# Expert batches of 6, 5, 3 and 2 groups in units of 128 rows, with the first layer's weights of a unit copied by ScalarE

## What is computed

```python
def _L0_gnn_ref(z, dist_matrix, W, B):
    msg = z @ W + B
    sens = exp(-(1.0 / r - 1.0 / MU) ** 2 / (2.0 * SIGMA ** 2))       # r = dist_matrix
    return where(dist_matrix < CUTOFF, sens, 0.0) @ msg

def _L0_ffn_ref(x, gate_w, gate_b, w1, b1, w2, b2, gamma, beta):      # H, F, E, K = 128, 256, 16, 2
    topk_vals, topk_idx = top_k(x @ gate_w + gate_b, K)
    topk_w = softmax(topk_vals, axis=-1)
    h = relu(einsum('bsh,ehf->bsef', x, w1) + b1)
    expert_out = einsum('bsef,efh->bseh', h, w2) + b2
    y = x + sum(topk_w * expert_out[topk_idx])
    return layernorm(y) * gamma + beta

x = x + _L0_gnn_ref(layernorm(x), adj, W, B)
x = x + _L0_ffn_ref(layernorm(x), ...)
```

## Time and profile before

| what | value |
|---|---|
| median of 3 runs | 1759.18 us (1758.34 to 1759.6) |
| the profiled execution | 1758.88 us, span 1757.1 us |
| PE busy | 1624.8 us, 92% |
| DVE busy | 1525.8 us, 87% |
| ACT busy | 1581.2 us, 90% |
| POOL busy | 430.1 us, 24% |
| HBM traffic | 194 GB/s over the span |

### The profile page before, as it was taken

The page is one execution under the profiler, slowest core; times in us unless marked ns, Lnnn a source line. Parts: engine busy times, 40 slices in busy tenths (PEclk is TensorE's granted clock), DMA queues, the critical chain, the costliest instruction groups (busy, mean ns, idle before and its releaser), DMA issues.

```text
span 1757.1 us, 23405 instructions
## 1 busy us (share of the span) xinstructions
PE 1624.8 (92%) x8178; PEld 1080.6 (61%) x8178; DVE 1525.8 (87%) x2278; ACT 1581.2 (90%) x1577; POOL 430.1 (24%) x309
## 2 busy tenths in 40 slices
PE   4889999999999999999999999999999999999840
PEld 3556666566656566656556656566656557999840
DVE  7999999999999999999999999999999994557876
ACT  5889999999999999999989999999999995666752
POOL 0000030303131313131304030303031301117775
PEclk9999999999999999999999999999999999999985
DMA  9447876667666666666867666667666842457653
GB/s 319 146 136 252 251 213 205 187 203 217 200 203 199 195 204 204 202 200 201 230 192 207 203 207 204 189 202 216 203 188 203 230 123 77 149 156 227 193 152 97
DMA packets 208500, 341.91 MB, mean 195 GB/s; under 512 B 18224, under 2 KB 65840, under 8 KB 208256
## 3 DMA queue, kind: packets, MB, share of 16 engines
q1 hardware_dynamic: 200064, 323.30, 61.9%
q0 software_dynamic: 8320, 17.12, 3.2%
HBM read 304.38 MB, written 35.98 MB: 194 GB/s over the span
## 4 chain that ended last, share of the span: by engine, by line
PE 44%; ACT 28%; DVE 12%; issue 11%; POOL 4%; DMA 1%; POOLq 0%; SPq 0%; DVEq 0%; ACTq 0%
PE acc L1033 22%; PE tp L1052 11%; ACT chunk L467 10%; ACT chunk L462 9%; ACT wT L473 8%; PE tp L1082 4%; PE tp L1095 4%; POOL chunk L446 4%; DVE chunk L595 4%; DVE chunk L589 4%; PE tp L1071 1%; PE misc L985 1%; DVE stats L601 1%; DVE msg L650 1%; DMA xs<-in_x_dram 1%
## 5 line engine op out<-in xcount | busy, mean ns | idle before, releaser
L1033 PE MATMUL acc<-wT,msg 128*128 128x512 f32 x2048 | 973.0, 598 | 16.2 <-DVE yT L681 16.2
L595 DVE SCALAR_TENSOR_TENSOR chunk<-chunk 128x2048 f32<-128x2048 f32 x256 | 585.6, 2287 | 98.2 <-ACT chunk L467 98.0
L1052 PEld LDWEIGHTS tp<-ident,chunk 128*128 128x128 f32 x4096 | 484.1, 142 | 226.2 <-issue 214.7
L473 ACT ACTIVATE wT<-tp 128x1024 f32<-128x1024 f32 x512 | 570.4, 1114 | 22.4 <-PE tp L1052 22.4
L589 DVE SCALAR_TENSOR_TENSOR chunk<-chunk 128x2048 f32<-128x2048 f32 x256 | 584.0, 2282 | 1.9 <-DMA chunk<-in_adj_dram 1.9
L1052 PE MATMUL tp<-ident,chunk 128*128 128x128 f32 x4096 | 538.5, 275 | 0.0
L462 ACT ACTIVATE chunk<-chunk 128x2048 f32<-128x2048 f32 x256 | 514.9, 2011 | 11.9 <-DVE chunk L589 11.9
L1033 PEld LDWEIGHTS acc<-wT,msg 128*128 128x128 f32 x2048 | 351.6, 192 | 267.7 <-issue 267.0
L467 ACT ACTIVATE chunk<-chunk 128x2048 f32<-128x2048 f32 x256 | 513.7, 2007 | 0.0
L418 POOL TENSOR_TENSOR pool_carrier<-pool_carrier 1x1 f32<-1x1 f32 x32 | 8.6, 270 | 1232.0 <-DVE row_now L766 1189.5
L428 POOL DMA_INDIRECT rows_in<-y,row_now x128 | 286.6, 2239 | 44.7 <-issue 44.7
(11 more groups left out here) (106 smaller groups left out, 574.8 us busy)
## 6 DMA issues: line engine op xcount, KB each, us to landing
chunk<-in_adj_dram SPq DMA_DIRECT2D x256, 1024.0 KB, 5.3
chunk<-rows_in SPq DMA_DIRECT2D x88, 128.0 KB, 2.1
rows_out<-chunk SPq DMA_DIRECT2D x88, 128.0 KB
y_kept<-y SPq DMA_DIRECT2D x16, 256.0 KB, 6.1
rows_in<-zeros SPq DMA_DIRECT2D x32, 128.0 KB
chunk<-y_kept SPq DMA_DIRECT2D x16, 256.0 KB, 3.4
out_dram<-chunk SPq DMA_DIRECT2D x16, 256.0 KB, 2.6
blobs<-in_L_ffn_w_dram SPq DMA_DIRECT2D x1, 2048.0 KB, 12.0
```

The source lines that it names most:

```text
L473: act.activation(wT[:, (g * PPG + m) % WSLOTS, :], tp[(g * PPG + m) % TSLOTS][:, :], ACT.Exp, scale=-2.0).then_inc(weighted, 1)
L595: dve.scalar_tensor_tensor(out=slot(c), in0=slot(c), scalar=2.0, in1=slot(c), op0=ALU.subtract, op1=ALU.mult).then_inc(squared, 1)
L1033: ins = pe.matmul(acc[:, :], msg[:, n, :], wT[:, (g * PPG + m) % WSLOTS, k * ROWS:(k + 1) * ROWS], start=(n == 0), stop=(n == 2 * PPG - 1))
L1052: ins = pe.transpose(tp[s % TSLOTS][:, t * ROWS + b * P:t * ROWS + (b + 1) * P], chunk[:, c % RING, b, j:j + P], ident[:, :])
```

## The change

There are four batches, of 6, 5, 3 and 2 groups, all in units of 128 rows, and a batch has 15 more units than its rows fill: 63, 55, 39 and 31, in all 188. There are three tables in the main phase, beside groups 7, 12 and 15. A unit's weights come to its slot by two engines: ACT copies the 256 columns of the first layer (`fetch_first`), DVE the other 386. Both run five units ahead, in 7 slots. PE's `hidden` waits for ACT's copy (`first_full`), `output` and ACT's `relu_hidden` for DVE's. There are 12 buffers for rows and 6 for results where there were 8 and 4. The gate's steps lie two units apart, and a combine begins every 11 iterations: 77, 88, 99, 110, 121, 132, 143, 154, 165, 176, 187, then 198, 209, 220, 231 and 242 with no units beside them.

```diff
-    BATCHES = (8, 6, 2)
-    TILES = (2, 2, 1)
+    BATCHES = (6, 5, 3, 2)
+    TILES = (1, 1, 1, 1)
...
-    UNITS = [K * n * ROWS // u + E for n, u in zip(BATCHES, UR)]
+    UNITS = [K * n * ROWS // u + E - 1 for n, u in zip(BATCHES, UR)]
...
-        SLOTS, RIN, RT, HT, RO, BACK, ZS, FIN = 4, 8, 3, 3, 4, 4, 3, 2
+        SLOTS, RIN, RT, HT, RO, BACK, ZS, FIN = 7, 12, 3, 3, 6, 4, 3, 2
...
-        GATE_PACE = 1
-        TABLE_AT, PADS_AT = 28, 47
+        GATE_PACE = 2
+        TABLE_AT, PADS_AT = 55, 74
         TAIL_TABLES = len(BATCHES) - 1
-        COMBINE_WAIT, COMBINE_PACE, COMBINE_LONG = 8, 6, 10
+        COMBINE_WAIT, COMBINE_PACE, COMBINE_LONG = 14, 11, 10
...
-                starts.append(max(at, starts[-1] + pace) if starts else at)
+                starts.append(max(at, starts[-1] + COMBINE_PACE) if starts else at)
...
+            def fetch_first(u):
+                b = batch_of(u)
+                if u == 0:
+                    act.wait_ge(weights_in, EXPERT_DMAS * 16)
+                if u == UNIT0[b]:
+                    act.wait_ge(table_ready, 2 * b + 2)
+                if u == UNIT0[b] or u % AT_ONCE == 0:
+                    upper = min(u // AT_ONCE * AT_ONCE + AT_ONCE, UNIT0[b + 1])
+                    _, values = nc.values_load_multi_w_load_instructions(
+                        e_tab[0:1, u:upper], engines=[mybir.EngineType.Activation], min_val=0, max_val=E - 1,
...
+                if u >= SLOTS:
+                    act.wait_ge(hid_full, u - SLOTS + 1)
+                act.activation(slots[u % SLOTS][:, W1:W1 + F], blobs[:, bass.ds(first_layers[u], 1), W1:W1 + F].rearrange("p a f -> p (a f)"),
+                               ACT.Copy).then_inc(first_full, 1)
...
                 act.wait_ge(hid_full, u + 1)
+                act.wait_ge(slot_full, u + 1)
...
+            for u in range(SLOTS - 2):
+                fetch_first(u)
             copy_rows(0)
...
                     relu_hidden(i + 1)
+                if i + SLOTS - 2 < NU:
+                    fetch_first(i + SLOTS - 2)
...
-                dve.tensor_copy(slots[u % SLOTS], blobs[:, bass.ds(experts[u], 1), :].rearrange("p a f -> p (a f)")).then_inc(slot_full, 1)
+                dve.tensor_copy(slots[u % SLOTS][:, W2:BLOB], blobs[:, bass.ds(experts[u], 1), W2:BLOB].rearrange("p a f -> p (a f)")).then_inc(slot_full, 1)
...
-                if i + 2 < NU:
-                    fetch(i + 2)
+                if i + SLOTS - 2 < NU:
+                    fetch(i + SLOTS - 2)
...
-                pe.wait_ge(slot_full, u + 1)
+                pe.wait_ge(first_full, u + 1)
...
                 pe.wait_ge(hT_ready, u + 1)
+                pe.wait_ge(slot_full, u + 1)
```

More of the change, by code:

```diff
@@ L211, in gnn_moe_kernel @@
         slot_full = sem("slot_full")
+        first_full = sem("first_full")
         hid_full = sem("hid_full")
@@ L230, in gnn_moe_kernel @@
         SETUP_MISC = 2
-        def batch_at(i):
-            return max(b for b in range(len(BATCHES)) if UNIT0[b] <= i)
-        GATE_PACE = 1
-        TABLE_AT, PADS_AT = 28, 47
+        GATE_PACE = 2
+        TABLE_AT, PADS_AT = 55, 74
         TAIL_TABLES = len(BATCHES) - 1
-        COMBINE_WAIT, COMBINE_PACE, COMBINE_LONG = 8, 6, 10
+        COMBINE_WAIT, COMBINE_PACE, COMBINE_LONG = 14, 11, 10
         starts = []
@@ L243, in gnn_moe_kernel @@
                 at = UNIT0[b + 1] + COMBINE_WAIT
-                pace = COMBINE_PACE if starts and UR[batch_at(starts[-1])] > P else COMBINE_LONG
-                starts.append(max(at, starts[-1] + pace) if starts else at)
+                starts.append(max(at, starts[-1] + COMBINE_PACE) if starts else at)
         LAST = starts[-1] + COMBINE_LONG + 2
@@ L433, in results_there @@
                 for i in range(RO):
-                    pool.wait_ge(ro_out[i], UNIT0[b + 1] // RO * 16)
+                    pool.wait_ge(ro_out[i], (UNIT0[b + 1] - i + RO - 1) // RO * 16)
             for b, n in enumerate(BATCHES):
@@ L520, in _ @@
                         guess(c + 3, (c + 3) % 2)
+            first_layers = {}
+            def fetch_first(u):
[8 more added lines that the diff above has]
+                        e_tab[0:1, u:upper], engines=[mybir.EngineType.Activation], min_val=0, max_val=E - 1,
+                        skip_runtime_bounds_check_because="a count of experts, clamped to the last one")
+                    first_layers.update(zip(range(u, upper), values))
+                if u >= SLOTS:
+                    act.wait_ge(hid_full, u - SLOTS + 1)
+                act.activation(slots[u % SLOTS][:, W1:W1 + F], blobs[:, bass.ds(first_layers[u], 1), W1:W1 + F].rearrange("p a f -> p (a f)"),
+                               ACT.Copy).then_inc(first_full, 1)
             def copy_rows(u):
@@ L551, in combine_slot @@
                     ins.then_inc(zn_ready, 1)
+            act.wait_ge(turned, (GROUPS - 1) * PPG + PPG - RING // 2 * PAIRS)
+            for u in range(SLOTS - 2):
+                fetch_first(u)
             copy_rows(0)
@@ L947, in _ @@
             dve.wait_ge(turned, (GROUPS - 1) * PPG + PPG - RING // 2 * PAIRS)
-            for u in range(2):
+            for u in range(SLOTS - 2):
                 fetch(u)
```

## The result

The changed kernel took 1770.37 us in the median of five runs (1766.69 to 1771.55) against 1759.18 (five runs too, 1757.78 to 1759.76): ratio 1.0059, 95% interval 1.0045 to 1.0074. It is **slower**, by 11.2 us between the medians and by 10.4 us by the ratio. The forecast was 1755.3, a little faster; 1770.37 lies within its range, which went up to 1772, but the change of direction was not forecast. The profiled execution spans 1768.4 us, 11.3 more than before.

What follows compares the result with a forecast made beforehand. ACT was taken to bound the main phase, the units' pace the two chains after it. Main phase +4.5, units 0.0, combines -8.4 sum to -3.9 us: 1755.3 us against 1759.18, range 1743 to 1772.

Steps and rivals of the forecast that it cites:

- SP's pace in the unit stage: Unit stage, SP's loads and stores: 1.07 us a unit up to iteration 77, then 1.25 beside combines.
- SP's queue is the bound: Rival, unit stage: SP's slack is used up early, 1.12 then 1.32 us a unit, 1767 us, slower; chance 0.20.
- 224.3 us: Unit stage: 188 units take what 120 took before, no gain and no loss.
- Main phase: Before the unit stage: one more table in a full group costs 4.5 us, bounds 3 and 6.
- Combines: Behind the last unit: six groups instead of seven, 53.5 us instead of 61.9, 8.4 us less.
- The new copy: Unit stage, ACT's copy of 256 first-layer columns: 0.31 us, making 0.97 us of ACT a unit.
- The dear copy: Rival, unit stage: ACT's copy of 256 columns costs 0.385 us or more, 1767 us, slower; chance 0.10.
- ACT alone paces: Rival, unit stage: SP's loads run ahead, ACT sets 1.03 then 1.20 us a unit, 1747 us; chance 0.25.
- The change does not do what it says: Rival, unit stage: ACT's copies precede its relus, PE's clock falls to 1.2 GHz, 40 us or more; chance 0.03.
- POOL: Gathers beside the combines: POOL alone would end at 1734 us, so it has come off the path.
- Table loads: Unit stage: 0.7 us for each of ACT's fifteen; loads last 1.1 us in the median on DVE and SP.

Runs made afterwards that it cites:

- everything that won: Changed kernel with paired stores, last batch's pads on POOL, all 642 columns fetched by DVE, a combine every 9 iterations: 1881.11, 1879.96 and 1880.9 us on slower chips.

## Why the prediction was wrong, point by point

- **The step that failed: SP's pace in the unit stage.** 1.00 us for store and load was right, and so was the order of the extras. But I took 1.07 us a unit for the first 77, on the ground that about 4 us of slack would carry half of the loss (SP's own sum was 1.12), and 1.25 beside combines, by spreading 16 pads, table loads and combine DMAs evenly over 110 units. Measured by DVE's adds, with the fill, the stage's first 77 iterations took 91.7 us where the forecast had 86.8 (+4.9), the other 110 took 151.7 for 137.5 (+14.2); together the 19.0. SP's slack did carry the first units: from the first add to the 41st it is 44.4 us, and 44.6 with SP relieved. DVE first waits for a store at 1522.90 us, for unit 42, and by the 77th add the changed kernel is 5.9 us behind the relieved one (89.1 for 83.2). Pads come one to a unit in a row: units 80 to 100 took 33.8 us, of which 20 x 1.25 = 25 were forecast, so 8.8 of the 14.2 lie in that fifth. Without the pads the same 20 units took 25.2. Six result buffers do not even that out: DVE waits as soon as six stores are behind. More of them were not tried.
- **The rival that came true** is the one that named this place: "SP's queue is the bound", 1767 us, 0.20. It had 1.12 and 1.32; measured, from the first add to the 77th, 1.17 (89.1 / 76, in which 2.5 us for the gate's products and the first gather lie too) and then 1.38 (151.7 / 110). Its condition was wrong: it was to decide only from 1.04 us for store and load on, and it decided at 1.00, by the extras. Its mechanism (pads, table loads and long issues together, DVE waiting for a result buffer) is what the waits show; for the stage it was 7.5 us short.
- **That 224.3 us came after all is luck.** With SP relieved the stage took 224.6 us, with 1.09 us a unit before combines (83.2 / 76, again with the gate's products) and 1.26 beside them (138.8 / 110). But the forecast's 1.07 and 1.25 were made from SP's cost, which is cut by 0.3 us a unit there. With SP out of the way the prediction's own sum for ACT alone is 210.3 + 5.5 = 215.8 us, 8.8 less than measured, and without ACT's copy the stage still took 221.9. So the terms behind SP were too low as well. ACT was busy for over 19 us in five of the eleven windows of 20 us from 1480 to 1700; how the 8.8 us divide among ACT, DVE, the rings and the table loads is open.
- **Main phase**: +4.5 forecast, +1.1 measured. With the change, the windows of the two groups with tables and of the last one, from one group's L703 copy to the next:

```profile
676.39:769.50 93.11, 88.36 (x398) 53.55 (x399) 88.53 (x103) 88.08 (x68) 19.08 (x9) 0.96 0.67 194
...
1118.74:1210.81 92.07, 86.66 (x399) 53.65 (x399) 87.52 (x103) 87.90 (x68) 19.07 (x9) 0.98 0.70 202
...
1385.24:1471.86 86.62, 84.67 (x382) 51.65 (x382) 69.66 (x99) 76.34 (x65) 11.24 (x9) 0.98 0.42 120
```

and of the last group before:

```profile
1381.11:1470.65 89.54, 85.05 (x384) 51.27 (x383) 70.13 (x97) 74.74 (x60) 9.91 (x9) 0.98 0.48 136
```

The two groups near 92 us came as said. The last is 2.9 us shorter. It is so in all versions with these batches (86.62, 86.63, and 85.71 with units of 256 rows), but with the old batches and ACT's copy (the run at 1806 us) it was 87.84, so up to 1.7 of the 2.9 us do not go with the batches. And 1.2 us are there at the first group (its L703 at 153.22 us, L681 at 154.44 before), ahead of anything that was changed. The +1.1 is not firm: in three profiles of one kernel, that with everything that won, the unit stage starts at 1468.99, 1473.74 and 1474.20 us. All profiles with units of 128 rows throughout have it below the 1475.4 of the forecast, so the term was too high, by how much is not known.
- **Combines**: -8.4 forecast, -8.8 measured, 8.4 us each, and the last waits for no gather. Right.
- **The new copy**: 0.31 us forecast. ACT's timeline (L535 is the copy, L544 the next row copy): 1499.85 to 1500.16 is 0.31. A whole unit, 1499.16 to 1500.16, is 1.00 without a wait that the profile shows, where the sum had 0.97; so ACT has no room there either. The dear copy falls. The Trainium skill's formula (ScalarE: Activation LUTs, section What ACT_TABLE_LOAD costs) gives an estimated 0.31 for it too: by that formula, the trace agrees.

```profile
1499.16 0.28 ACT L544 ACTIVATE chunk<-tp 128x128 f32<-128x128 f32 x1
1499.34 0.63 ACT L554 ACTIVATE chunk<-tp,chunk 128x128 f32<-128x128 f32 x2
1499.85 0.42 ACT L535 ACTIVATE chunk<-blobs 128x256 f32 x1
1500.16 0.28 ACT L544 ACTIVATE chunk<-tp 128x128 f32<-128x128 f32 x1
```

- **ACT alone paces** (0.25): it would have needed SP to run ahead, and SP did not. With SP relieved it was still too low, as said.
- **The change does not do what it says** (0.03): the granted clock was 1.00 in most windows of 20 us and 0.91 in two. Each of those two holds one short stretch at half speed, the 1.2 GHz level, from about 1592 and from about 1622 us on. Ahead of the first PE had waited 1.07 us for DVE's add, and DVE then waited 1.74 us for a store:

```profile
1590.00:1592.00 2.00, 0.93 (x9) 0.77 (x8) 0.51 (x2) 1.62 (x7) 1.55 (x2) 1.00 0.52 138
1592.00:1594.00 2.00, 2.00 (x12) 2.00 (x11) 1.29 (x8) 0.66 (x3) 1.52 (x4) 0.53 0.91 250
```

So the clock did fall, but not by the order of ACT's work, which the rival had named, and for two short stretches in place of a large part of the stage.
- **POOL**: said to be off the path, and it was at the end: no combine waited for a gather. It stood still for 18.9 us for the second batch, a wait that I had not looked for.
- **Table loads**: 0.7 us each beyond their cover. Medians of about 1.1 us were right, but the longest were 2.2 to 2.4 us against 1.35 in the earlier trace rows. The loads with the change, on DVE and ACT, then on SP. What makes one long stays open, and no run gives the price of the 0.7 us term by itself.

```profile
L914 DVEq TENSOR_LOAD <-e_tab x15: 313/1191/2417, 1457.1 to 1695.1; - x15
L529 ACTq TENSOR_LOAD <-e_tab x15: 279/1092/2290, 1466.8 to 1695.4; - x15
```

```profile
L333 SPq TENSOR_LOAD <-r_tab x15: 313/989/2242, 1446.0 to 1691.2; - x15
```

## What to carry to other kernels

When work is cut into smaller pieces, recount the queue that starts the transfers: its price is by the piece, not by the byte (SP was held 0.43 us by most stores of 64 KB, and 0.38 or 0.43 us by most of 128 KB). Cost a queue stretch by stretch, with the DMAs that fall on one unit added up there, and compare with the slack in units of the ring; an average over the stage hides the stretch that decides. Relief for that queue (two results in one store, pads by an idle engine) was worth more here (18.8 us of the stage) than the arithmetic that the change had moved between engines (1.2 to 2.7 us).

## What the runs showed of the hardware that was not expected

**Two kinds of chip, as far as was seen.** On the first two chips of the experiments the kernel before takes 1758 us, on three later ones 1880 to 1881. Each chip was seen once, and the slow ones came last, so that it is the chip and not the time or the machine is not shown. One kernel (the two reliefs) was seen on both. Its windows on a chip of the first kind:

```profile
589.70:677.04 87.34, 85.41 (x404) 53.06 (x404) 80.14 (x88) 87.31 (x69) 19.45 (x9) 1.00 0.68 201
1500.00:1520.00 20.00, 19.49 (x175) 19.28 (x174) 12.78 (x63) 19.09 (x77) 0.00 (x0) 1.00 0.47 133
1570.00:1590.00 20.00, 18.64 (x155) 17.54 (x153) 16.98 (x70) 19.30 (x76) 15.69 (x18) 1.00 0.69 192
```

and on the slower kind:

```profile
589.70:677.04 87.34, 87.00 (x404) 54.03 (x404) 80.17 (x88) 87.31 (x68) 19.44 (x9) 0.98 0.66 196
1500.00:1520.00 20.00, 19.69 (x177) 19.48 (x176) 12.40 (x61) 19.12 (x76) 0.00 (x0) 1.00 0.40 112
1570.00:1590.00 20.00, 4.41 (x16) 3.05 (x15) 0.68 (x3) 2.14 (x7) 15.39 (x19) 0.50 0.19 53
```

A plain group of the main phase takes 87.34 us on both, and the first units run at the same pace. From 1560 to 1600 us, where POOL's gathers follow one another without a break, the second chip does none to three units in 10 us in place of seven to nine, with PE's clock at 0.50, the 1.2 GHz level; where POOL issues none (1650 to 1670) it does seven to nine. It is slow too where POOL scatters the last group's rows, before any gather: 10 units from 1520 to 1540 us where the first chip does 18. POOL itself keeps its pace in both. In the main phase, where POOL scatters as well, nothing of that size is lost. ACT's timeline there has waits of 5 to 7 us behind matmuls of PE that, by the profile, had ended:

```profile
1578.73 0.28 ACT L578 ACTIVATE chunk<-tp 128x128 f32<-128x128 f32 x1 [5.43 <-remote]
1585.77 0.63 ACT L588 ACTIVATE chunk<-tp,chunk 128x128 f32<-128x128 f32 x2 [6.77 <-remote]
```

What it is that holds PE's signals or PE itself back was not tried, and that POOL's indirect transfers cause it is only a coincidence in time so far. It bears on the verdict: the version that gains 0.35% on one kind of chip loses 0.5% on the other.

**A load of register values costs by the value**: in the median 1.02 us on ACT where the middle load brings 16 and 2.13 where it brings 28. The spread is from 0.28 to 3.7 us; the shortest may be the loads at the batches' starts, of which one brings a single number.
